# Packed rows of the edge loop stored as late columns of all batches, then early ones

## What is computed

```
pre_u = x @ W1[:256]            pre_v = x @ W1[256:]
hidden[b,u,v,:] = relu(pre_u[b,u,:] + pre_v[b,v,:] + b1)
S[b,u,v] = sigmoid(hidden[b,u,v,:] @ W2 + b2)
a = einsum('buv,bud->bvd', S * adj, x)
m = einsum('uv,bud->bvd', adj, x) * x
out = beta1*x + beta2*(a @ Wa + ba) + beta3*(m @ Wm + bm)
```

## Time and profile before

| | |
|---|---|
| median of 3 runs | 3654.01 us (3653.74 to 3662.95) |
| profiled execution | 3660.8 us, its span 3659.0 us |
| mean granted clock | 0.976 |
| TensorE busy | 3409.4 us, 93% |
| VectorE busy | 2720.7 us, 74% |
| ScalarE busy | 2335.8 us, 64% |
| GpSimd busy | 1734.5 us, 47% |
| edge loop, first to last product | 1173.0 to 3105.5 us |
| HBM read and written | 444.01 and 256.18 MB, mean 191 GB/s |

### The profile page before, as it was taken

The page is one execution under the profiler, slowest core; times in us unless marked ns, Lnnn a source line. Parts: engine busy times, 40 slices in busy tenths (PEclk is TensorE's granted clock), DMA queues, the critical chain, the costliest instruction groups (busy, mean ns, idle before and its releaser), DMA issues. The chain is left out here.

```text
span 3659.0 us, 56051 instructions
## 1 busy us (share of the span) xinstructions
PE 3409.4 (93%) x14232; PEld 2632.6 (72%) x14232; DVE 2720.7 (74%) x4866; ACT 2335.8 (64%) x14066; POOL 1734.5 (47%) x2306
## 2 busy tenths in 40 slices
PE   3999999999897899999999999999999999589998
PEld 2666565666565688878788888888888887478887
DVE  3555555655544799999999999999999999354444
ACT  0211211121111699989999999999999998578786
POOL 1211111211110556666666666566766665466664
PEclk9999999999998999999999999999999999789999
DMA  5666666666657866567666676666756653967674
GB/s 194 247 218 228 239 219 243 238 232 236 227 198 194 193 153 144 141 156 169 154 146 139 150 182 164 156 149 144 175 143 155 153 130 75 321 223 245 217 245 165
DMA packets 342570, 685.80 MB, mean 187 GB/s; under 512 B 38718, under 2 KB 252840, under 8 KB 319400
## 3 DMA queue, kind: packets, MB, share of 16 engines
q1 hardware_dynamic: 286704, 587.95, 56.2%
q0 software_dynamic: 21504, 53.31, 4.8%
q10 hardware_dynamic: 34032, 40.90, 3.2%
HBM read 444.01 MB, written 256.18 MB: 191 GB/s over the span
## 5 line engine op out<-in xcount | busy, mean ns | idle before, releaser
L1194 ACT ACTIVATE junk<-psum_a 128x128 f32<-128x128 f32 x6144 | 1606.7, 292 | 218.3 <-PE psum_a L1098 144.1
L1194 ACT ACTIVATION_READ_ACCUMULATOR junk<-psum_a 128x1 f32 x6144 | 1366.1, 223 | 0.0
L1139 DVE TENSOR_REDUCE group_sum<-psum_d 128x56 f32<-128x896 f32 x1024 | 1113.2, 1087 | 83.6 <-PE psum_d L1098 41.8
L1098 PE MATMUL psum_d<-v_t,pk 128*128 128x512 f32 x1920 | 754.6, 393 | 0.0
L1243 POOL DMA_INDIRECT sum_dram<-total,idx_all x512 | 505.9, 988 | 228.1 <-POOL total L1254 124.1
L1513 PE MATMUL z_psum<-hWa_all,masked 128*128 128x256 f32 x2048 | 471.3, 395 | 73.2 <-DVE masked L1497 48.1
L1097 PE MATMUL psum_d<-first_u,pk 128*128 128x512 f32 x1280 | 508.6, 397 | 23.6 <-DMA pk<-pick_dram 10.6
L971 POOL TENSOR_TENSOR own<-whole 128x256 f32<-128x256 f32 x128 | 113.0, 883 | 874.5 <-DVE own_mixed L769 537.3
L1097 PE MATMUL psum_d<-u_t,pk 128*128 128x512 f32 x1280 | 503.8, 394 | 13.1 <-issue 11.9
L727 ACT COPY whole<-ring 128x258 f32<-128x258 f32 x128 | 47.9, 374 | 723.5 <-PE ring L641 709.2
L1513 PEld LDWEIGHTS z_psum<-hWa_all,masked 128*128 128x128 f32 x2048 | 406.6, 199 | 137.9 <-issue 50.3
(11 more groups left out here) (213 smaller groups left out, 5098.5 us busy)
## 6 DMA issues: line engine op xcount, KB each, us to landing
sum_dram<-zero SPq DMA_DIRECT2D x128, 512.0 KB, 4.0
rows_dram<-split SPq DMA_DIRECT2D x128, 512.0 KB, 3.2
pk<-pick_dram SPq DMA_DIRECT2D x512, 128.0 KB
u_t<-rows_dram SPq DMA_DIRECT2D x64, 1024.0 KB
raw<-sum_dram SPq DMA_DIRECT2D x64, 1024.0 KB, 5.0
first_u<-rows_dram SPq DMA_DIRECT2D x62, 1024.0 KB
whole_dram<-whole SPq DMA_DIRECT2D x128, 256.0 KB, 3.4
pick_dram<-first_v SPq DMA_DIRECT2D x128, 256.0 KB, 3.4
```

What stands on the lines that cost most here:

```text
L1098: return nc.tensor.matmul(dst, pk[n % PKS][:, SLOTS + at:SLOTS + at + P], part(v_t[n % VG][:], b, LB), start=False, stop=True)
L1139: nc.vector.tensor_reduce(out_[:, :, 1:EG], in_[:, :, GW:LATE].rearrange("p b (g k) -> p b g k", k=GW), AX, ALU.add, apply_absolute_value= ...
L1194: last = nc.scalar.activation(junk[:, a % RING_A, k * LATE:(k + 1) * LATE], psum_a[a % RING_A][:, k * LATE:(k + 1) * LATE], ACT.Abs, accum ...
```

## The change

rows_dram, and with it u_t, v_t, first_u and first_v, holds in each row first the late columns of all batches (2048 values), then the early columns of all batches (2048 values). `early` and `late` now give four batches' columns that lie behind one another. store_rows writes each batch's 256 columns in two pieces, load_first loads two pieces. whole_dram keeps its layout; what reads it (left_rows, rows_m) uses whole_early and whole_late, which are the former early and late. No instruction of VectorE, ScalarE, GpSimd or TensorE is added or removed.

```diff
--- before.py
+++ after.py
@@ -504,8 +504,8 @@
                     def store_rows(b, t):
                         g = b * NT + t
                         sp.wait_ge(low_ready, g + 1)
-                        sp.dma_start(rows_dram[t * P:(t + 1) * P, :, :, b * D:(b + 1) * D].rearrange("p w q k -> p (w q) k"),
-                                     split[:, g % RW, :, :, :].rearrange("p w q k -> p (w q) k")
+                        sp.dma_start(rows_dram[t * P:(t + 1) * P, :, :, :].rearrange("p w q (s b k) -> p (w q) s b k", s=2, b=B)[:, :, :, b, :],
+                                     split[:, g % RW, :, :, :].rearrange("p w q (s k) -> p (w q) s k", s=2)
                                      .bitcast(fp32)).then_inc(rows_stored[g % RW], 16)
                         sp.dma_start(whole_rows[t * P:(t + 1) * P, :, b * D:(b + 1) * D],
                                      whole[:, g % RW, :, 0:D]).then_inc(rows_stored[g % RW], 16)
@@ -520,12 +520,12 @@
                                      pick[p_ % RPK].bitcast(fp32)).then_inc(pick_stored[p_ % RPK], 16)
 
                     def load_first(i, b, end):
-                        at, to = b * D, end * D
+                        at, to = b * LATE, end * LATE
                         for q in range(HALVES):
-                            sp.dma_start(first_u[q * UB:(q + 1) * UB, at:to].bitcast(fp32),
-                                         rows_dram[0:UB, 0, q, at:to]).then_inc(first_loaded[i], 16)
-                            sp.dma_start(first_v[q * VB:(q + 1) * VB, at:to].bitcast(fp32),
-                                         rows_dram[0:VB, 1, q, at:to]).then_inc(first_loaded[i], 16)
+                            sp.dma_start(first_u[q * UB:(q + 1) * UB, :].rearrange("p (s c) -> p s c", s=2)[:, :, at:to].bitcast(fp32),
+                                         rows_dram[0:UB, 0, q, :].rearrange("p (s c) -> p s c", s=2)[:, :, at:to]).then_inc(first_loaded[i], 16)
+                            sp.dma_start(first_v[q * VB:(q + 1) * VB, :].rearrange("p (s c) -> p s c", s=2)[:, :, at:to].bitcast(fp32),
+                                         rows_dram[0:VB, 1, q, :].rearrange("p (s c) -> p s c", s=2)[:, :, at:to]).then_inc(first_loaded[i], 16)
 
                     for b in range(B):
                         pairs = pairs_of(b)
@@ -1003,10 +1003,17 @@
         QUARTER = ROW // 4
         LD, LA = 5, 6
 
+
         def early(rows_, b, n):
+            return rows_[:, ROW // 2 + b * LATE:ROW // 2 + (b + n) * LATE].rearrange("p (b k) -> p b k", k=LATE)
+
+        def late(rows_, b, n):
+            return rows_[:, b * LATE:(b + n) * LATE].rearrange("p (b k) -> p b k", k=LATE)
+
+        def whole_early(rows_, b, n):
             return rows_.rearrange("p (b s k) -> p b s k", s=2, k=LATE)[:, b:b + n, 1, :]
 
-        def late(rows_, b, n):
+        def whole_late(rows_, b, n):
             return rows_.rearrange("p (b s k) -> p b s k", s=2, k=LATE)[:, b:b + n, 0, :]
 
         def v_loads(k, jj):
@@ -1173,11 +1180,11 @@
                                 waits(dve, left_d, w * LD)
                             if step < 4:
                                 some = slice(step * LB, (step + 1) * LB)
-                                pure(left_sum[:, lt, some, :], early(rows_, step * LB, LB))
-                                sign_mixed(left_mixed[:, some, :], early(rows_, step * LB, LB), LB).then_inc(left_d, 1)
+                                pure(left_sum[:, lt, some, :], whole_early(rows_, step * LB, LB))
+                                sign_mixed(left_mixed[:, some, :], whole_early(rows_, step * LB, LB), LB).then_inc(left_d, 1)
                             else:
                                 dve.wait_ge(left_d, w * LD + 4)
-                                lates(left_late[:, lt, 3 * LB:4 * LB], late(rows_, 3 * LB, LB))
+                                lates(left_late[:, lt, 3 * LB:4 * LB], whole_late(rows_, 3 * LB, LB))
                                 nc.vector.tensor_reduce(left_sum[:, lt, :, 0], left_mixed[:], AX, ALU.add).then_inc(left_d, 1)
 
                 @block.scalar
@@ -1407,7 +1414,7 @@
                                 dve.wait_ge(m_gathered, 16 * 2 * TILES)
                                 for i in range(TILES):
                                     link(TT(rows_m[i][:], rows_m[i][:], cols_m[i][:], ALU.add))
-                                    early_m, late_k = early(rows_m[i][:], 0, B), late(rows_m[i][:], 0, B)
+                                    early_m, late_k = whole_early(rows_m[i][:], 0, B), whole_late(rows_m[i][:], 0, B)
                                     link(nc.vector.tensor_reduce(sums_m[:, :, 1:EG], early_m[:, :, GW:LATE].rearrange("p b (g k) -> p b g k", k=GW),
                                                                  AX, ALU.add, apply_absolute_value=True))
                                     link(STT(out=mixed_m[:], in0=early_m[:, :, 0:GW], scalar=0.0,
```

## The result

The changed kernel takes 3668.53 us (median of 20 runs, 3655.67 to 3683.21) against 3654.81 for the kernel before (20 runs, 3645.3 to 3666.2). The ratio is 1.0035, 95% interval 1.0023 to 1.0048: 13 to 14 us slower. The profiled execution has a span of 3667.2 us against 3659.0.

The account below looks back on a forecast made before the run. TensorE's time per product was taken to bound the edge loop. Edge loop 0, pick delay +5 and loads 0.2 summed to +5 us on the 3654.0 median: 3659 us, range 3600 to 3690 (the forecast's own 3645 to 3680).

Parts of the forecast that it names:

- The edge term: Edge loop: the 16 ns per product above its columns do not come from the breaks; 0 us, ends 0 and -135.
- two readings of L601: One-run product's 8.8 ns excess: grows with columns, breaks cost nothing; or fixed per product, three breaks at most 3.4 ns.
- rivals 1 and 2: Edge loop: breaks cost the whole excess, 3550 us, chance 0.10; or part of it, 3614 us, chance 0.18.
- The store term: First stretch: row stores of 512 B pieces take 0.2 us more each, delaying pick stores queued behind; +5 us.
- The issue itself: 0: SP's queue, first stretch: a store's issue time does not follow its run count, so more pieces add 0 us.
- TensorE's share: First stretch: of VectorE's 8 us added wait for pick stores, TensorE feels 56.4/126.0, say 4 us.
- Rival 3: SP's queue, first stretch: row stores take up to 1.5 us more, delaying picks; 3685 to 3711 us, chance 0.12.

Follow-up runs that it names:

- one-run kernel: Kernel before, only the edge products' moving operand exchanged for one run of 512 columns instead of four of 128: 3657.06 us against 3656.61, ratio 1.0001.
- stores-only kernel: Changed kernel with its 512 B stores, batches placed so that edge products read four runs of 128 again: 3669.82 us, ratio 1.0042 to the kernel before.
- two other kernels with small pieces: Changed kernel with products reading four runs again, 3669.82 us; kernel before with row stores of 256 B pieces, 3690.22 us.
- picks first: Pick tables stored before the packed rows on SP's queue: 3566.71 us in the changed kernel, 3562.57 us in the kernel before.
- bf16 kernel: Kernel before, edge products reading their operands as bf16, one run of 512 columns, everything else kept: 3582.73 us, ratio 0.979.

## Why the prediction was right

**The edge term, 0 us: right.** The step that carried it was L601, a single-pass product with one run and an excess of its own size. The one-run kernel and the stores-only kernel confirm both halves. Of the two readings of L601, growing with columns or fixed per product, the result fits the first: nothing, not 3.4 ns, went with the breaks. No run varied the number of columns. The weight I gave rivals 1 and 2, 0.28 together, was for a cost that is not there.

**The store term, +5 us: mechanism right, size off.** It measured 13 to 14 us in the runs, and 9 to 16 in the first stage of the profiles, where I had put 2 to 10. The place was the one named, pick stores behind row stores, but two factors of the sum were too small. The first is the time per store. I had 0.2 us, of which the engines' share rests on 9 ns for a packet under 512 B, a value that no row gives; with the 30 ns per piece that the rows allow at most, a pair costs 12 ns more and a store 0.4 us. The delay measured 0.3 us (the landing of row and pick stores), 12.5 us over the 38 waits. "The issue itself: 0" was right of L507's own issue and wrong of those behind it, in which the same 0.3 us stand. The second factor is TensorE's share. I let it feel less than half of VectorE's added wait; its wait grew by 9.9 us where VectorE's grew by 12.5, and in the two other kernels with small pieces by 15.6 of 17.7 and 27.4 of 34.8.

Those 9.9 us are not all of the 16.1 by which the start of the loop moved in the one pair of profiles. Part of it is the spread of the start, told above. The clock explains none of it that can be seen: it was low for 47.8 us of the first stage instead of 30.7, but among the kernels with the stores of before two had it low for 41.0 us and started the loop at 1176.2 and 1176.5, and one with 30.7 started at 1176.0.

**Rival 3** had this place and too high a price: its upper end, a piece of 512 B as dear as one of 1 KB, would have given 1.5 us per store; the landing grew by 0.3 us. The result lies between my forecast and its middle, inside the forecast's own range, and over the 11 us that can be told from no change. That range left room on both sides of the sum; it does not make the sum's 5 us right.

**By the Trainium skill**, "TensorE: Matmul & The Clock Gate", Back-to-back issue gap, the gap after an isolated product of 512 columns is 215.8 ns, and some 131 ns in a steady stream. Here the steady stream of bf16 products has 216, which agrees with the first figure and not with the second; the fp32r runs have 229, with one run of columns or four, and agree with neither. Its "DMA: Bandwidth & Descriptors", Specifications, calls 512 B enough for line rate: 3.5 against 3.2 us to landing says nearly, and the kernel lost on what stood behind it in the queue.

**Left open.** In every profile with small pieces whose order was the old one, the first products on the second u_t came 6 us later after the loop's start (65.6 us after it, 59.2 before), and with picks first it was so too (64.0 against 56.8). The bf16 kernel with large pieces had 64.7, so the pieces are not the only thing that moves it. The loop as a whole took 1932.0 to 1933.1 us in the kernels with the stores of before and fp32r products in runs of 64 columns or more, and 1935.2 to 1937.8 in the three with small pieces. So some 3 to 5 us of the loss stand in the loop. Why these products start later was not tried.

## What to carry to other kernels

Before a layout is changed for longer reads, find a product in the trace that already reads one run with the same type: if it carries the same excess, the breaks are not the cause. When a store gets more pieces, count what stands behind it in its queue and who waits for that; here moving the waited-for store ahead of one that nobody waits for so soon was worth 2.4%, seven times what the pieces cost. The kernel before with that move, at 3562.57 us, is the version to keep.

## What I had not expected of the hardware

- A product of 512 columns with 4-byte operands takes 229 ns at 2.4 GHz in a burst, and one with 2-byte operands 216; with the moving 2-byte values at a step of 4 bytes it takes 226.
- Runs of 64 fp32 columns or more read as well as one run; runs of 32 take 237 ns and runs of 16 take 243.
- A DMA with 1024 pieces issues in the same 0.52 us as one with 512, and the DMAs issued behind it take longer: a mean of 0.97 us instead of 0.83 for a pick store, and a median of 677 ns instead of 640 for the whole store (1198 behind pieces of 256 B).
